# Transposing the right half of a graph's edge counts by DMA instead of on TensorE, in a four-layer graph network

## The chip, the cores and the metric

The kernel runs on one core of one Trainium2 chip. The metric is the device time of one execution in microseconds (us), lower is better. The core has five engines that run side by side, each with its own instruction stream: TensorE (PE in the profile; its weight loads are PEld), VectorE (DVE), ScalarE (ACT), GpSimd (POOL) and SyncE (SP), which here does nothing but issue DMAs. The engines are ordered among themselves by semaphores alone. TensorE writes to PSUM, eight banks of 128 x 512 float32; DVE and ACT read PSUM, a DMA does not.

## The reference, cut to what matters

Four graph layers over 1024 nodes of 512 features, each followed by a residual and a layer norm, with 16384 edges `(src, dst)`. The first layer, which the change touches, builds an adjacency matrix from the edges, made symmetric, and multiplies with it three times:

```python
def _L0_gnn_ref(x, edge_index, W, b, diffusion_weights):
    h = x @ W + b
    row, col = (edge_index[0], edge_index[1])
    adj = jnp.zeros((N, N), dtype=h.dtype)
    adj = adj.at[row, col].set(1.0)
    adj = adj.at[col, row].set(1.0)
    adj = adj + jnp.eye(N, dtype=h.dtype)
    row_sum = adj.sum(axis=1, keepdims=True)
    adj = adj / jnp.maximum(row_sum, 1.0)
    out = diffusion_weights[0] * h
    cur = h
    for i in range(STEPS):          # 3
        cur = adj @ cur
        out = out + diffusion_weights[i + 1] * cur
    return jax.nn.relu(out)

x = _layernorm(x + _L0_gnn_ref(x, edge_index, ...))
x = _layernorm(x + _L1_gnn_ref(x, W, b, src, dst, 1024))   # segment sum over edges, then @ W.T + b
x = _layernorm(x + _L2_gnn_ref(x, wc, wn, bias, edge_index))
x = _layernorm(x + _L3_gnn_ref(x, edge_index, Ws, Wb, a_w, a_b))   # attention, 8 heads
```

## The kernel before

Everything stays in SBUF. The edges become a dense matrix of counts: `c32` (float32, 8 tiles of 128 source nodes by 1024 destination nodes) is filled by one-hot matmuls of TensorE whose windows VectorE adds (L780, L1238), until about 66.9 us. Beside this TensorE computes `h = x @ W0` (L759), in float32.

Then comes the stage that the change touches, from 66.9 to 87.6 us:

- **Casts.** `c32` is cast to float16 in `cst` in pieces. The left half of the columns (0 to 511) is cast first, by ACT for tiles 0 to 2 (L517, which the profile shows under its helper's line, L453) and by DVE for tiles 3 to 7 (L1277). The right half (columns 512 to 1023) follows: tile 7 by ACT, tiles 0 and 1 by DVE (L1307), tiles 5 and 6 by ACT, tiles 2 to 4 by DVE (L1324). The semaphores `cst_act` and `cst_dve` count these casts, to 4 each.
- **Transposes.** `ct_block(t)` (L847) is eight transposes of 128x128 on TensorE (L853), which put column block `t` of all eight tiles into one PSUM bank (three banks in rotation); ACT copies that bank to `cts[:, t, :]` (L453, `cts<-ps`) and raises `cts_ready`. `cts` is the transposed count matrix in float16. Layer 3 reads it again, much later (L976).
- **Adjacency.** For `t` = 0 to 7 DVE waits for `cts_ready`, compares (L1318: an entry is 1 where either count is above 0, with the row sum), and adds the identity on the diagonal (L1322), which raises `adj_ready`. After tile 7 it computes the inverse degrees (L1325, L1326, semaphore `inv_r`) and the attention's weights (L1329 to L1331, semaphore `wa_lo`).
- **First multiplication, four banks.** TensorE goes over `j` = 0 to 7: it waits for `adj_ready` of tile `j` and issues 8 matmuls of 128x512 (L868) into the banks of tiles 6, 7, 3 and 4. Blocks 0 to 2 of the transposes are issued before this loop, block 3 before `j` = 0, and blocks 4 to 7 behind the matmuls of `j` = 1 to 4.
- **First multiplication, the other four banks** (L879, 64 matmuls), after `cts_ready` 8 and `wa_lo` 1. Then the second (L889, 128 matmuls) and third (L898) multiplications, and the later layers.

SP issues DMAs in the order of its program. After all of `h` is done it loads the weight matrices of the later layers, 1 MB each, into two staging halves: W1T and wc at once, wn and W3 as POOL frees the halves (`w_lo`, L395). ACT splits each into a high and a low part (`split_hi`, L453, `xTs<-xTs` and `big<-xTs`), from `inv_r` on, W1 and wc before it evicts the first multiplication. Later in the program SP issues 32 transposing DMAs (L340), each from one 128x512 float16 tile into four 128x128 blocks.

All of it is written out by hand: no scheduler moves anything. The order around the change is that of the code below.

Of the kernel before, what the change touches and what calls it, by code (L numbers as in the profile page):

```python
# [26 lines left out]
P = 128  # L27
N = 1024
D = 512
E = 16384  # L30
NT = N // P
# [19 lines left out]
ZERO_ACT = 6  # L51
CAST_COLS = ((0, 256), (256, 512), (512, 1024))
CT_BANKS = (0, 1, 5)
WINDOW_BANKS = (0, 1, 6, 7)

WSCALE = 64.0
# [40 lines left out]
def build(nc, x, xT, src, dst, W0, b0, dw, W1T, b1, wc, wn, b2, W3, W3T, b3, b3T, aw, ab, out):  # L97
    with ExitStack() as ctx:
# [10 lines left out]
        cst = sb("cst", [P, NT, N], F16)  # L109
        cts = sb("cts", [P, NT, N], F16)  # L110
# [147 lines left out]
        S = Semaphores()  # L258
# [38 lines left out]
        @block.sync  # L297
        def _(sp):
            sp.dma_start(e_dst, dst.rearrange("(g e) -> g e", e=GROUP)).then_inc(S["edges"], 16)
            sp.dma_start(e_src, src.rearrange("(g e) -> g e", e=GROUP)).then_inc(S["edges"], 16)  # L300
            sp.dma_start(first_i[:, 0, :], dst.rearrange("(a g e) -> a g e", a=1, e=GROUP)[:, :, 0],
                         allow_slow_non_contiguous=True).then_inc(S["edges"], 16)
            sp.dma_start(dwb[:], dw.rearrange("(a d) -> a d", a=1).broadcast_to([P, STEPS + 1])).then_inc(S["dw_in"], 16)
            sp.dma_start(w0raw, W0.rearrange("(k p) n -> p k n", p=P)).then_inc(S["w_in0"], 16)
            for half in range(2):
                nodes = slice(half * HALF, (half + 1) * HALF)
                sp.dma_start(xT32[:, :, nodes], xT.rearrange("(k p) n -> p k n", p=P)[:, :, nodes]).then_inc(S[f"xT_in{half}"], 16)
            sp.dma_start(w3t, W3T.rearrange("(k p) n -> p k n", p=P)).then_inc(S["w_in5"], 16)
            sp.dma_start(xcur[:], x.rearrange("(t p) d -> p t d", p=P)).then_inc(S["x_in"], 16)
            sp.dma_start(b0w, b0.rearrange("(a d) -> a d", a=1).broadcast_to([P, D])).then_inc(S["small_in"], 16)  # L310
            for i, b in enumerate((b1, b2, b3)):
                sp.dma_start(bb[:, i, :], b.rearrange("(a d) -> a d", a=1).broadcast_to([P, D])).then_inc(S["small_in"], 16)
            sp.dma_start(wbc[:], b3T).then_inc(S["small_in"], 16)
            sp.dma_start(abb[:], ab.rearrange("(a h) -> a h", a=1).broadcast_to([P, H])).then_inc(S["small_in"], 16)
            sp.dma_start(abc[:], ab.rearrange("(h a) -> h a", a=1)).then_inc(S["small_in"], 16)

            sp.wait_ge(S["const_ready"], 5)
            step = VCOL + H + 2
            flat = abT[:].rearrange("p k c -> p (k c)")
            for q in range(2):  # L320
                for u in range(2):
                    c0 = VCOL * u + q
                    sp.dma_start(flat[q * DH:(q + 1) * DH, c0:c0 + 3 * step + 1:step],
                                 aw.rearrange("(j q) (u p) -> q u p j", q=2, p=DH)[q, u],
                                 allow_slow_non_contiguous=True).then_inc(S["small_in"], 16)

            sp.wait_ge(S["h_done"], NT)
            for n, w in enumerate((W1T, wc, wn, W3)):
                if n >= 2:
                    sp.wait_ge(S["w_lo"], n - 1)  # L330
                sp.dma_start(stage[:, n % 2], w.rearrange("(k p) n -> p k n", p=P)).then_inc(S[f"w_in{n + 1}"], 16)
            for layer in range(1, 3):
                for t in range(NT):
                    name = ("xT_even", "xT_odd")[t % 2]
                    n = (layer - 1) * NT + t
                    sp.wait_ge(S["x_lo"], layer * NT + t + 1)
                    if n >= 2:
                        sp.wait_ge(S[name], n // 2 * TURNED)
                    for v in range(2):
                        sp.dma_start(xTs[:, v, :, t * P:(t + 1) * P], cur[:, 1, v, t, :],  # L340
                                     transpose=True).then_inc(S[name], 16)
            sp.wait_ge(S["uT_in"], 1)
            sp.dma_start(u_rows.rearrange("h (t p) -> (h t) p", p=P), uT).then_inc(S["u_kept"], 16)
            sp.wait_ge(S["u_kept"], 16)
            sp.wait_ge(S["wx_done"], NT)
            for h in range(2):
                sp.dma_start(uf[:, h], u_rows[h:h + 1].broadcast_to([P, N])).then_inc(S[f"uf_in{h}"], 16)
            for t in range(NT):
                if t in NORM_ACT:
                    sp.wait_ge(S["out_act"], NORM_ACT.index(t) + 1)  # L350
                else:
                    sp.wait_ge(S["out_dve"], NORM_DVE.index(t) + 1)
                sp.dma_start(out.rearrange("(t p) d -> t p d", p=P)[t], xcur[:, t, :]).then_inc(S["out_done"], 16)
            sp.wait_ge(S["out_done"], 16 * NT)
# [96 lines left out]
        def _(act):  # L451
# [66 lines left out]
                copy(cst[:, 0:CA, c0:c1], c32[:, 0:CA, c0:c1]).then_inc(S["cst_act"], 1)  # L518
            c0, c1 = CAST_COLS[2]
            copy(cst[:, 7:NT, c0:c1], c32[:, 7:NT, c0:c1]).then_inc(S["cst_act"], 1)  # L520
            for t in range(NT):
                act.wait_ge(S["ct_done"], t + 1)
                copy(cts[:, t, :], bank16(CT_BANKS[t % 3])).then_inc(S["cts_ready"], 1)
                if t == 2:
                    copy(cst[:, 5:7, c0:c1], c32[:, 5:7, c0:c1]).then_inc(S["cst_act"], 1)
# [64 lines left out]
            with act.Fori(0, NT // 2 - 1) as r:  # L590
                for i in (1, 0):
                    t = r * 2 + (2 - i)
# [12 lines left out]
            with act.If(flag(act, 2)):  # L605
# [23 lines left out]
                for a, n in enumerate(RELAYED):  # L629
                    h, j = n // NT, n % NT  # L630
# [83 lines left out]
        def _(pe):  # L714
# [48 lines left out]
            def quad(q):  # L763
# [7 lines left out]
                for w in (2 * q, 2 * q + 1):  # L771
                    pe.wait_ge(S["key_hot"], w + 1)
                    if w >= len(WINDOW_BANKS):
                        pe.wait_ge(S["win_free"], w - len(WINDOW_BANKS) + 1)
                    for c in (w % 2 * NC, w % 2 * NC + 1):
# [50 lines left out]
            with pe.If(flag(pe, 0)):  # L826
# [3 lines left out]
                with pe.Fori(0, NT) as a:  # L830
                    for b in range(2):
                        mm(ps[:, b, :], sel[:, H, :], iota_n[0:H, 0:HALF], start=True, stop=False)
                    with pe.Fori(0, NC * NG) as e:
                        n = a * (NC * NG) + e
# [12 lines left out]
            def ct_block(t):  # L847
                pe.wait_ge(S["cst_act"], (1, 2, 4)[chunk_of(t)])
                pe.wait_ge(S["cst_dve"], (1, 2, 4)[chunk_of(t)])
                if t >= 3:  # L850
                    pe.wait_ge(S["cts_ready"], t - 2)
                for j in range(NT):
                    ins = pe.transpose(bank16(CT_BANKS[t % 3])[:, j * P:(j + 1) * P], cst[:, j, t * P:(t + 1) * P], id16[:])  # L853
                ins.then_inc(S["ct_done"], 1)
# [7 lines left out]
            for j in range(NT):  # L862
                if j == 0:
                    ct_block(3)
                pe.wait_ge(S["adj_ready"], j + 1)
                for t in ORDER[0:OUTER]:
                    for v in range(2):
                        ins = mm(ps[:, t, :], adj[:, j, t * P:(t + 1) * P], cur[:, 0, v, j, :],  # L868
                                 start=j == 0 and v == 0, stop=j == NT - 1 and v == 1)
                    if j == NT - 1:  # L870
                        ins.then_inc(S["step_done"], 1)
                if 0 < j < NT - 3:
                    ct_block(j + 3)
            pe.wait_ge(S["cts_ready"], NT)
            pe.wait_ge(S["wa_lo"], 1)
            for t in ORDER[OUTER:NT]:
                for j in range(NT):
# [279 lines left out]
        def _(dve):  # L1157
# [74 lines left out]
            def add_window(w, first):  # L1232
                m = window(w // 2)
                dve.wait_ge(S["win_done"], w + 1)
                if w:
                    dve.wait_ge(S["win_free"], w)
                cells = c32[:, :, bass.ds(first.with_bounds(min_val=0, max_val=N - m), m)]
                tt(cells, cells, ps[:, WINDOW_BANKS[w % 4], 0:NT * m].rearrange("p (a w) -> p a w", w=m),  # L1238
                   ALU.add).then_inc(S["win_free"], 1)
# [41 lines left out]
            with dve.If(flag(dve, 0)):  # L1281
# [9 lines left out]
                with dve.Fori(0, NT) as a:  # L1291
                    with dve.Fori(0, CHUNKS) as e:
                        n = a * CHUNKS + e
# [13 lines left out]
            dve.tensor_copy(cst[:, 0:2, c0:c1], c32[:, 0:2, c0:c1]).then_inc(S["cst_dve"], 1)  # L1307

            for t in range(NT):
                dve.wait_ge(S["cts_ready"], t + 1)  # L1310
                if t == 0:
                    dve.wait_ge(S["cst_dve"], 3)
                    dve.wait_ge(S["cst_act"], 2)
                elif t == 2:
                    dve.wait_ge(S["cst_dve"], 4)
                elif t == 5:
                    dve.wait_ge(S["cst_act"], 4)
                stt(adj[:, t, :], cst[:, t, :], -1.0, cts[:, t, :], ALU.mult, ALU.is_lt,  # L1318
                    accum_out=deg[:, t:t + 1]).then_inc(S["adj_sum"], 1)
                dve.wait_ge(S["adj_sum"], t + 1)  # L1320
                diag = adj[:, t, t * P:(t + 1) * P]
                tt(diag, diag, id16[:], ALU.add).then_inc(S["adj_ready"], 1)  # L1322
                if t == 1:
                    dve.tensor_copy(cst[:, 2:5, c0:c1], c32[:, 2:5, c0:c1]).then_inc(S["cst_dve"], 1)  # L1324
# [61 lines left out]
            for k in range(1, STEPS):  # L1386
# [13 lines left out]
                for pos, t in enumerate(ORDER):  # L1400
                    n = (k - 1) * NT + pos + 1
# [79 lines left out]
            with dve.Fori(0, NT // 2 - 2) as r:  # L1481
                for i in (1, 0):
                    t = r * 2 + (2 - i)
# [278 lines left out]
```

## Time and profile before

| | us |
|---|---|
| median of 3 runs | 403.72 (403.42 to 404.16) |
| the profiled execution's own time | 403.67 |
| its span, first to last instruction | 401.8 |
| TensorE busy in the span | 370.4 (92%) |
| VectorE busy | 278.4 (69%) |
| ScalarE busy | 230.0 (57%) |
| GpSimd busy | 93.7 (23%) |
| chain that ended last: share of TensorE / VectorE / ScalarE | 74% / 14% / 3% |

The time of an execution is 1.9 us more than its span, so a change of the span is read as the same change of the time. The page gives busy time by engine; the chain of waits, followed back from the last instruction, tells which engine set the pace in which stretch; the timelines of single engines give the start and length of each instruction, and in brackets how long the engine sat idle before it and who released it. L numbers are lines of the kernel before.

### The profile page before, as it was taken

To read this page: it belongs to the slowest core of one execution; us is meant where nothing else is said; L and a number is where in the kernel's file an instruction comes from. 1 tells how busy PE (TensorE), PEld (TensorE's weight loads), DVE (VectorE), ACT (ScalarE), POOL (GpSimd) and SP (SyncE) were. 2 spreads that over 40 slices of the span, in tenths; PEclk is the share of its full clock that TensorE was granted. 3 is DMA by queue.
4 is the path that set the end of the run, shared out by engine and by line. 5 is a ranking of instruction groups with operands and counts; after the bars stand their busy time and mean duration, and the time that the engine had idled before them with its cause. 6 is when DMAs were issued, how large, how long until landed. Compare 5 with 4: busy or idle time off the path is not lost.

```text
span 401.8 us, 7998 instructions
## 1 busy us (share of the span) xinstructions
PE 370.4 (92%) x2704; PEld 216.0 (54%) x2704; DVE 278.4 (69%) x603; ACT 230.0 (57%) x390; POOL 93.7 (23%) x87
## 2 busy tenths in 40 slices
PE   1799889999999999999999999999798999999990
PEld 1254346444444444444444444444346889999990
DVE  7769998946996677024653222555798688999984
ACT  9789875566822145312562111246444999999444
POOL 4520000019940066500594000133100000012110
PEclk9999999999999999999999999999999999999996
DMA  5950004104100000000243000033202122210005
GB/s 180 390 178 2 1 0 160 52 0 148 64 0 2 1 0 3 2 0 0 42 91 78 0 2 2 2 76 79 54 1 63 46 68 93 97 64 2 4 3 212
DMA packets 27447, 22.71 MB, mean 57 GB/s; under 512 B 19536, under 2 KB 19728, under 8 KB 27408
## 3 DMA queue, kind: packets, MB, share of 16 engines
q1 hardware_dynamic: 26544, 19.06, 15.9%
q10 hardware_dynamic: 864, 3.15, 2.4%
q8 instruction: 23, 0.38, 0.4%
q14 instruction: 16, 0.13, 0.1%
HBM read 15.87 MB, written 2.13 MB: 45 GB/s over the span
## 4 chain that ended last, share of the span: by engine, by line
PE 74%; DVE 14%; issue 5%; ACT 3%; DVEq 2%; ACTq 0%
PE ps L726 15%; PE ps L1084 14%; PE ps L935 7%; PE ps L976 7%; PE ps L889 7%; PE ps L898 7%; PE ps L1025 7%; DVE c L1238 4%; PE ps L879 3%; PE ps L759 3%; PE ps L868 3%; DVE big L1473 2%; DVE adj L1219 1%; PE ps L780 1%; DVEq L1238 1%
## 5 line engine op out<-in xcount | busy, mean ns | idle before, releaser
L726 PE MATMUL ps<-big,xTs 128*128 128x512 f16 x384 | 84.4, 379 | 3.0 <-DVE cts L1460 3.0
L726 PEld LDWEIGHTS ps<-big,xTs 128*128 (+1 forms) x384 | 37.0, 98 | 47.0 <-issue 3.5
L635 ACT ACTIVATE big<-big,uvt 128x1024 bf16<-128x1024 f32 x55 | 59.0, 1153 | 0.0
L425 POOL TENSOR_TENSOR big<-xcur,big x24 | 27.8, 1157 | 119.6 <-ACT xcur L546 119.0
L545 ACT ACTIVATE big<-xcur,nmr,rstd x24 | 19.6, 815 | 38.8 <-DVE nmr L1344 38.8
L759 PE MATMUL ps<-big,xTs 128*128 128x512 f32 x64 | 35.3, 648 | 0.0
L453 ACT ACTIVATE big<-ps 128x512 f16<-128x512 f32 (+2 forms) x17 | 9.8, 574 | 39.9 <-PE ps L726 30.0
L1238 DVE TENSOR_TENSOR c<-c,ps 128x80 f32 (+31 forms) x64 | 23.3, 364 | 9.7 <-PE ps L780 5.6
L395 POOL TENSOR_TENSOR big<-xTs,big 128x2048 f16<-128x2048 f32 x4 | 16.3, 4086 | 58.8 <-ACT big L453 58.8
L1025 PE MATMUL ps<-big,cst 128*128 128x260 f16 x256 | 29.8, 275 | 0.0
L780 PE MATMUL ps<-adj,cts 128*128 128x80 f16 (+31 forms) x128 | 21.3, 271 | 8.9 <-DVE c L1238 4.8
L436 POOL TENSOR_TENSOR xcur<-xcur,c 128x512 f32<-128x512 f32 x6 | 7.1, 1182 | 94.6 <-DVE c L1557 94.6
L780 PEld LDWEIGHTS ps<-adj,cts 128*128 128x128 f16 x128 | 11.3, 108 | 31.7 <-issue 16.6
L935 PE MATMUL ps<-cst,big 128*128 128x512 f16 x128 | 27.8, 379 | 0.4 <-issue 0.4
L898 PE MATMUL ps<-big,adj 128*128 128x512 f16 x128 | 27.9, 379 | 0.0
L889 PE MATMUL ps<-big,adj 128*128 128x512 f16 x128 | 27.8, 379 | 0.0
L976 PE MATMUL ps<-big,cts 128*128 128x512 f16 x128 | 27.8, 379 | 0.0
L1025 PEld LDWEIGHTS ps<-big,cst 128*128 128x128 f16 x256 | 24.3, 96 | 4.8
L476 ACT ACTIVATE cts<-iota_lo,early 128x128 f16<-128x128 f16 x80 | 25.4, 393 | 0.4
L1219 DVE TENSOR_TENSOR adj<-adj,early 128x160 f16<-128x160 f16 (+31 forms) x64 | 22.3, 391 | 0.1
L453 ACT ACTIVATE big<-ps,invdeg 128x512 f16<-128x512 f32 x16 | 10.3, 688 | 19.1 <-PE ps L889 14.9
L935 PEld LDWEIGHTS ps<-cst,big 128*128 128x128 f16 x128 | 12.5, 98 | 15.7 <-issue 0.9
(206 smaller groups left out, 651.8 us busy)
## 6 DMA issues: line engine op xcount, KB each, us to landing
big<-u_rows ACTq DMA_DIRECT2D x6, 512.0 KB, 3.7
xTs<-in_xT SPq DMA_DIRECT2D x2, 1024.0 KB, 9.4
xcur<-in_x SPq DMA_DIRECT2D x1, 2048.0 KB, 17.8
out<-xcur SPq DMA_DIRECT2D x8, 256.0 KB, 2.5
big<-in_W SPq DMA_DIRECT2D x1, 1024.0 KB, 6.1
cts<-in_W3T SPq DMA_DIRECT2D x1, 1024.0 KB, 13.1
xTs<-in_W1T SPq DMA_DIRECT2D x1, 1024.0 KB, 5.4
xTs<-in_wc SPq DMA_DIRECT2D x1, 1024.0 KB, 8.2
```

The costliest lines, as they stand in the source:

```text
L425: pool.tensor_tensor(cur[:, 1, 1, t, :], xcur[:, t, :], cur[:, 1, 0, t, :], ALU.subtract).then_inc(S["x_lo"], 1)
L635: act.activation(above[:, a % AHEAD, :], uf[:, h % 2], ACT.Relu, scale=BIG, bias=vb[:, j, h:h + 1]).then_inc(S["above_in"], 1)
L726: return mm(bank, lhs(k)[a], rhs(k)[b], start=start and k == 0 and n == 0, stop=stop and k == KT - 1 and n == 2)
L759: ins = mm(bank, xT32[:, k, t * P:(t + 1) * P], w0raw[:, k, :], start=k == 0, stop=k == KT - 1)
L780: ins = mm(ps[:, WINDOW_BANKS[w % 4], 0:n], left, hot_key[:, r, w % 2 * NC * n:(w % 2 + 1) * NC * n].rearrange("p (k c) -> p k c", c=NC)[: ...
L889: ins = mm(ps[:, t, :], adj[:, j, t * P:(t + 1) * P], cur[:, 1, v, j, :], start=n == 0 and v == 0, stop=n == NT - 1 and v == 1)
L898: ins = mm(ps[:, t, :], adj[:, j, bass.ds(t * P, P)], cur[:, 0, v, j, :], start=n == 0 and v == 0, stop=n == NT - 1 and v == 1)
L935: ins = mm(ps[:, half * KT + k, :], cur[:, 1, v, j, k * P:(k + 1) * P], c[:, j, half * HALF:(half + 1) * HALF], start=c is cst and j == 0 ...
L976: ins = mm(ps[:, t, :], c[:, j, bass.ds(t * P, P)], cur[:, 0, v, j, :], start=c is cts and j == 0 and v == 0, stop=c is parts[-1] and j == ...
L1025: ins = mm(ps[:, DENSE_BANK[i], 0:4 * (DH + 1)], cst[:, j, t * P:(t + 1) * P], yh[:, j, v, 4 * half:4 * half + 4, DH + 1:YW], start=j == 0 ...
L1084: ins = mm(o, cz[h % CZ][:, j, t * P:(t + 1) * P], yh[:, j, v, h, :], start=j == 0 and v == 0, stop=j == NT - 1 and v == 1)
L1238: tt(cells, cells, ps[:, WINDOW_BANKS[w % 4], 0:NT * m].rearrange("p (a w) -> p a w", w=m), ALU.add).then_inc(S["win_free"], 1)
```

## The change

Tiles 0 to 3 of `cts` are made as before. Tiles 4 to 7, that is the right half of the columns of `cst`, are made by eight transposing DMAs, one for each tile `j` of `cst`: each reads 128x512 float16 of `cst[:, j]` and writes block `j` of the four tiles `cts[:, 4:8]`. SP issues them between the loads of W1T and of wc, in the order 0, 1, 7, 5, 6, 2, 3, 4, each group behind the cast that writes its source. TensorE's blocks 4 to 7 and ACT's four copies of them are gone. DVE waits ahead of tile 4 for all eight DMAs, and TensorE waits for `cts_ready` 4 instead of 8 ahead of the other four banks. The load of wc stands behind the eight DMAs.

```diff
+CT_PE = 4
@@ SP
             sp.wait_ge(S["h_done"], NT)
-            for n, w in enumerate((W1T, wc, wn, W3)):
+            def load(n):
                 if n >= 2:
                     sp.wait_ge(S["w_lo"], n - 1)
+                w = (W1T, wc, wn, W3)[n]
                 sp.dma_start(stage[:, n % 2], w.rearrange("(k p) n -> p k n", p=P)).then_inc(S[f"w_in{n + 1}"], 16)
+
+            def turn_counts(j):
+                sp.dma_start(cts[:, CT_PE:NT, j * P:(j + 1) * P], cst[:, j, CT_PE * P:N], transpose=True).then_inc(S["ct_turned"], 16)
+
+            load(0)
+            sp.wait_ge(S["cst_dve"], 3)
+            turn_counts(0)
+            turn_counts(1)
+            sp.wait_ge(S["cst_act"], 3)
+            turn_counts(7)
+            sp.wait_ge(S["cst_act"], 4)
+            turn_counts(5)
+            turn_counts(6)
+            sp.wait_ge(S["cst_dve"], 4)
+            turn_counts(2)
+            turn_counts(3)
+            turn_counts(4)
+            for n in range(1, 4):
+                load(n)
@@ ACT
-            for t in range(NT):
+            for t in range(CT_PE):
                 act.wait_ge(S["ct_done"], t + 1)
                 copy(cts[:, t, :], bank16(CT_BANKS[t % 3])).then_inc(S["cts_ready"], 1)
@@ TensorE
-                if 0 < j < NT - 3:
-                    ct_block(j + 3)
-            pe.wait_ge(S["cts_ready"], NT)
+            pe.wait_ge(S["cts_ready"], CT_PE)
@@ VectorE
             for t in range(NT):
-                dve.wait_ge(S["cts_ready"], t + 1)
+                if t < CT_PE:
+                    dve.wait_ge(S["cts_ready"], t + 1)
+                elif t == CT_PE:
+                    dve.wait_ge(S["ct_turned"], NT * 16)
```

The order of SP's instructions, from the load of W1T on (semaphores waited for in brackets; xTs is the staging memory). Before:

```order
L331 DMA xTs<-in_W1T 128x4x512 [waits h_done]
L331 DMA xTs<-in_wc 128x4x512
L331 DMA xTs<-in_wn 128x4x512 [waits w_lo]
L331 DMA xTs<-in_W 128x4x512 [waits w_lo]
L340 DMA_TRANSPOSE xTs<-big 128x4x128 [waits x_lo]
```

With the change:

```order
L333 DMA xTs<-in_W1T 128x4x512 [waits h_done]
L336 DMA_TRANSPOSE cts<-cst 128x4x128 [waits cst_dve]
L336 DMA_TRANSPOSE cts<-cst 128x4x128
L336 DMA_TRANSPOSE cts<-cst 128x4x128 [waits cst_act] x2
L336 DMA_TRANSPOSE cts<-cst 128x4x128
L336 DMA_TRANSPOSE cts<-cst 128x4x128 [waits cst_dve]
L336 DMA_TRANSPOSE cts<-cst 128x4x128 x2
L333 DMA xTs<-in_wc 128x4x512
L333 DMA xTs<-in_wn 128x4x512 [waits w_lo]
```

Eight transposing DMAs of the same shape as the later ones now stand between W1T and wc.

The order of TensorE's instructions, from the matmuls of `j` = 1 on. Before:

```order
L868 MATMUL ps<-big,adj 128x512 [waits adj_ready]
L868 MATMUL ps<-big,adj 128x512 x7
L853 MATMUL ps<-id16,cst 128x128 [waits cts_ready,cst_dve,cst_act]
L853 MATMUL ps<-id16,cst 128x128 x7
L868 MATMUL ps<-big,adj 128x512 [waits adj_ready]
L868 MATMUL ps<-big,adj 128x512 x7
L853 MATMUL ps<-id16,cst 128x128 [waits cts_ready,cst_dve,cst_act]
L853 MATMUL ps<-id16,cst 128x128 x7
```

With the change, where L889 is the line that was L868 and L898 the one that was L879:

```order
L889 MATMUL ps<-big,adj 128x512 [waits adj_ready]
L889 MATMUL ps<-big,adj 128x512 x7
L889 MATMUL ps<-big,adj 128x512 [waits adj_ready]
L889 MATMUL ps<-big,adj 128x512 x7
L898 MATMUL ps<-big,adj 128x512 [waits wa_lo,cts_ready]
```

The four blocks of transposes are gone from between the groups of eight matmuls, which now follow one another up to the first matmul of L898.

## Rows read from the trace of the kernel before

**Rows 1.** The page: the span, and busy time by engine
```profile
span 401.8 us, 7998 instructions
...
PE 370.4 (92%) x2704; PEld 216.0 (54%) x2704; DVE 278.4 (69%) x603; ACT 230.0 (57%) x390; POOL 93.7 (23%) x87
```

**Rows 2.** The chain of waits, 66.9 to 90 us: start us, us, engine, what
```profile
75.69 1.90 PE ps L868 x8
77.59 0.45 PE ps L853 x8
78.04 1.73 PE ps L868 x8
...
82.39 5.18 PE ps L868 x24
```

**Rows 3.** The chain of waits after 87 us, its longest pieces
```profile
87.57 13.81 PE ps L879 x64
101.38 27.63 PE ps L889 x128
```

**Rows 4.** Timeline of DVE: start, us, line, out<-in, [idle before <-releaser]
```profile
69.23 0.68 DVE L1307 CAST cst<-c 128x1024 f16<-128x1024 f32 x1
...
72.82 1.22 DVE L1324 CAST cst<-c 128x1536 f16<-128x1536 f32 x1
...
75.55 1.22 DVE L1318 SCALAR_TENSOR_TENSOR adj<-cst,cts 128x1024 f16<-128x1024 f16 x1
...
76.96 1.22 DVE L1318 SCALAR_TENSOR_TENSOR adj<-cst,cts 128x1024 f16<-128x1024 f16 x1
...
78.22 0.22 DVE L1322 TENSOR_TENSOR adj<-adj,id 128x128 f16<-128x128 f16 x1
79.13 1.23 DVE L1318 SCALAR_TENSOR_TENSOR adj<-cst,cts 128x1024 f16<-128x1024 f16 x1 [0.69 <-ACT cts L453]
...
83.48 1.23 DVE L1318 SCALAR_TENSOR_TENSOR adj<-cst,cts 128x1024 f16<-128x1024 f16 x1 [0.68 <-ACT cts L453]
...
85.81 0.33 DVE L1331 TENSOR_TENSOR wa<-abT,wa 128x160 f16<-128x160 f32 x1
```

**Rows 5.** Timeline of ACT, the same columns
```profile
71.62 1.06 ACT L453 ACTIVATE cst<-c 128x1024 f16<-128x1024 f32 x1
...
75.67 1.02 ACT L453 ACTIVATE cts<-ps 128x1024 f16<-128x1024 f16 x1 [2.07 <-PE ps L853]
...
85.38 1.91 ACT L453 ACTIVATE xTs<-xTs 128x2048 f32<-128x2048 f32 x1 [1.93 <-DVE invdeg L1326]
```

**Rows 6.** SP's transposing DMAs, L340, 196 to 216 us: ns min/median/max, starts
```profile
L340 SPq DMA_TRANSPOSE xTs<-big x15: 1189/1267/1313, 196.2 to 215.1; - x15
...
DMA to landing us min/median/max: 2.4/2.5/2.5
```

**Rows 7.** The same line, 279 to 283 us
```profile
L340 SPq DMA_TRANSPOSE xTs<-big x3: 1188/1268/2392, 278.2 to 281.3; - x3
```

**Rows 8.** A stretch: length, busy by engine, granted clock, DMA share, GB/s
```profile
197.50:198.00 0.50, 0.50 (x4) 0.26 (x3) 0.24 (x2) 0.00 (x0) 0.40 (x1) 1.00 1.03 209
```

**Rows 9.** DMA issues by what they load: KB each, us from issue to landing
```profile
xTs<-in_W1T SPq DMA_DIRECT2D x1, 1024.0 KB, 5.4
xTs<-in_wc SPq DMA_DIRECT2D x1, 1024.0 KB, 8.2
```

**Rows 10.** Stretches after TensorE's last matmul, the columns of rows 8
```profile
391.70:394.50 2.80, 0.00 (x0) 0.00 (x0) 2.56 (x13) 1.96 (x6) 0.00 (x0) 1.00 0.67 249
394.50:395.00 0.50, 0.00 (x0) 0.00 (x0) 0.47 (x2) 0.50 (x2) 0.00 (x0) 0.81 0.54 193
395.00:396.00 1.00, 0.00 (x0) 0.00 (x0) 0.89 (x5) 0.71 (x2) 0.00 (x0) 0.50 0.12 47
```

**Rows 11.** TensorE's float32 matmuls, L759, before 23 us and after
```profile
L759 PE MATMUL ps<-big,xTs x7: 682/1061/1220, 14.9 to 22.7; 128*128 128x512 f32 x7
...
L759 PE MATMUL ps<-big,xTs x53: 590/592/682, 22.7 to 60.0; 128*128 128x512 f32 x53
```

## The prediction

> **What bounds the kernel now.** I read the page first: TensorE is busy for 370.4 of 401.8 us [rows 1], so time is lost or won where TensorE waits. The chain of waits then says where it doesn't. From 75.69 us on, the chain is TensorE alone: groups of eight L868 matmuls of 1.73 us, between them three blocks of transposes of 0.45 us (77.59 us is the first of them), then 5.18 us of L868 without a block [rows 2], then L879 from 87.57 and L889 from 101.38 us without a gap [rows 3]. Whatever moves the end of L868 therefore moves the whole rest. Of a block's 0.45 us, three lie on the chain. The fourth (block 4) comes ahead of 75.69, where TensorE waits for VectorE anyway.
>
> VectorE's timeline shows who feeds TensorE. Tile 3 starts at 75.55 and tile 4 at 76.96, 1.41 us later, with no wait. From tile 5 on each waits some 0.69 us for ScalarE's copy (79.13, 83.48) [rows 4]. ScalarE's copy takes 1.02 us, and ScalarE sits idle for 2.07 us ahead of it [rows 5]. So VectorE could take a tile each 1.41 us, and TensorE takes one each 1.73 us: the pace is TensorE's, transposes included.
>
> **What the change removes.** TensorE loses four blocks; three on the chain are 3 x 0.45 = 1.35 us. ScalarE loses four copies, 4 x 1.02 = 4.1 us, worth nothing: it was idle before them, and its next work (the split of W1 at 85.38) waits for the inverse degrees, that is for VectorE [rows 5]. VectorE loses its waits of 0.69 us ahead of tiles 5 to 7. All of that counts only if the DMAs have landed when VectorE comes to tile 4, at 76.96 us.
>
> **What it adds: eight transposing DMAs.** The same kernel has the nearest row one could wish: 15 issues of L340 in one stretch, each from 128x512 float16 into four blocks at the same stride as here. Each holds SP for 1189 to 1313 ns, median 1267; from the first start, 196.2, to the last, 215.1 us, the 14 intervals are 18.9 us, 1.35 each, with short waits for GpSimd's tiles among them; one lands 2.4 to 2.5 us after its issue begins [rows 6]. I take an interval of 1.30 us, between the bare issue and the interval with waits.
>
> - The first waits for `cst_dve` 3, the L1307 cast, which ends at 69.23 + 0.68 = 69.91 us [rows 4]. Issue at 69.95.
> - The later sources are no brake: ScalarE's cast ends near 72.7 [rows 5], VectorE's L1324 at 74.04 [rows 4], while by SP's own pace the fourth DMA starts at 73.9 and the sixth at 76.5.
> - The eighth starts at 69.95 + 7 x 1.30 = 79.05 and lands at 79.05 + 2.5 = 81.55 us.
>
> VectorE waits at tile 4 for all eight. It stands ready at 76.96 and starts at 81.6, 4.6 us late. From the start of a tile to the end of its identity add it takes 78.22 + 0.22 - 76.96 = 1.48 us [rows 4], so TensorE gets tile 4 at 83.1. It has finished tile 3 at 75.69 + 1.90 + 1.73 = 79.3, so it stands idle for 3.8 us. Then come four groups of eight at 1.73 us (VectorE's 1.41 us keeps ahead), 6.9 us: L868 ends at 90.0 instead of 87.57. **The balance is +2.4 us**: 3.8 us of new wait less 1.35 us of transposes.
>
> **Is any of it taken up behind?** L879 waits for `wa_lo`, which came at 85.81 + 0.33 = 86.1, 2.7 us after tile 7 began at 83.48 [rows 4]. Tile 7 now begins at 81.6 + 3 x 1.41 = 85.8, so `wa_lo` comes at 88.5, ahead of 90.0. Nothing is gained or lost there. ScalarE's and GpSimd's weight splits, and VectorE's first corrections, all hang on the inverse degrees and move by 85.8 - 83.5 = 2.3 us, as TensorE does within 0.1; so L889, which needs them, meets what it met before. Behind it TensorE's chain has no gap [rows 3] in which a delay could vanish.
>
> **The moved load.** W1T's load goes first and landed after 5.4 us; wc, issued close behind it, after 8.2 [rows 9]. Now wc is issued behind the eighth transpose, at 80.4, and lands by 88.6 even at 8.2 us. ScalarE first splits W1 (two steps of 1.91 us from 85.38 + 2.3 = 87.7 [rows 5]) and needs wc at 91.5. Cost nothing, with 3 us of cover; if the load took over 11 us, the ScalarE evictions behind it would be late. wn and W3 wait for GpSimd as before and move with it. W1T has landed by 69.4 at that rate, before the first transpose.
>
> **Sum.** 403.67 (the profiled execution's own time, span 401.8 and 1.9 around it) + 2.4 = 406.1 us. The median of the runs, 403.72, is the same to 0.05. Bounds of the known terms: at the shortest issue, 1.189, and the shortest landing, 2.4, the last lands at 80.7 and the loss is 1.5; at 1.35 it lands at 81.9 and the loss is 2.8. One issue of 2392 ns stands in another stretch [rows 7]; one such here would add 1.1. This case alone holds 405.0 to 407.2.
>
> **Rivals.**
>
> *The clock falls in the new gap.* At the end of the kernel TensorE's last matmul ends near 391.7; the granted clock is still 1.00 up to 394.5, averages 0.81 in the next half microsecond and is 0.50 (1.2 GHz) after 395 [rows 10]. That is a fall some 3.1 us after the last matmul. The new gap is 3.8 us, the longest inside the kernel. Against it: the fall need not come at the same distance each time, and the gap ends only 0.7 us later. The price: in the kernel's first stretch float32 matmuls took 1061 ns where they take 592 later, from 14.9 to 22.7 us, 7.8 us of half rate though TensorE was at work [rows 11]. If the clock comes back 3 to 7.8 us after 83.1, half of that is lost, 1.5 to 3.9 us; I take 2.5, which gives 408.6 us. The Trainium skill (TensorE: Matmul & The Clock Gate, Part 1) has the clock go back to its lower level after idleness, and warns of waits for DMAs inside a kernel. Taken as sure, it would give 408.6 in place of 406.1; the trace has the fall only behind the last matmul, so I leave it a chance of 1 in 4.
>
> *The issue is not the pace, and it is faster.* In the burst from 197.5 to 198.0 us a transpose moved 209 GB/s at a DMA share of 1.03 [rows 8], so 128 KB took some 0.6 us, and the engines rested for the other half of each 1.30 us. If SP issued at the DMAs' pace, the last three (sources ready at 74.04) would start by 75.3 and land by 77.8: VectorE would be 0.8 us late, TensorE hardly, and all 1.35 us would be won, 402.3 us. The point at which it turns is worked back from the sum: the last landing at 81.55 - 2.4 = 79.15 us, an interval of 0.95 us. Against it stands the row of 15 with a minimum of 1.189 [rows 6]. The Trainium skill (Advanced Engine Details and Errata, X-Bar Transpose) calls transposing DMAs as fast as ordinary ones, with 350 to 400 GB/s to be expected. By that figure eight take 3 us and the time would be 402.3; the measured interval speaks against it. Chance 4 in 100.
>
> *Part of the delay is taken up or the landing comes near 79.1*: between 402.9 and 404.5, without a mechanism that the rows show. 6 in 100.
>
> *The change doesn't do what it says*: excluded by the order of instructions, which has eight transposing DMAs on SP, and four blocks gone from TensorE.
>
> **How the numbers follow.** The forecast has 65 in 100, the clock 25, the faster case 4, no change 6. Differences under 0.2% (0.8 us) can't be told from none: faster is below 402.9, slower above 404.5. Faster 0.04, same 0.06, slower 0.90. The range goes from just under the bound of the fastest issue, 404.9, into the clock's case, to 409.2, and leaves out the first two small cases and the far end of the clock's: about 2 in 10. The likeliest time is 406.1.
>
> **What would show it.** Right: eight transposing DMAs from about 70 us at 1.3 us each; VectorE idle for 4.6 us ahead of tile 4 with a DMA as releaser; one TensorE gap of some 3.8 us ahead of the fifth group of L868, no other change until the end, everything from L879 on 2.4 us later. Wrong in size: a granted clock under 1.00 between 82 and 91 us, or eight L868 matmuls taking more than 1.73 us. Wrong in kind: issue intervals below 0.95 us, VectorE's wait short, or a first transpose that starts long after 70 us, which would mean that SP waits for something I don't see.

## The result, and the profile after

The changed kernel takes 409.16 us (median of 4 runs, 408.61 to 409.63) against 403.69 (403.42 to 404.16): a ratio of 1.0137, interval 1.0125 to 1.0149. It is slower by 5.5 us, where the forecast had 2.4. The profiled execution took 408.77 us and its span is 406.9 us; before it was 403.67 and 401.8. Between these two the whole difference, 5.1 us, is in the span, and the sums below are worked out from them; the other 0.4 us is the distance of the profiled execution from the median.

The page of the changed kernel, its span and busy time by engine:

```profile
span 406.9 us, 7933 instructions
...
PE 371.9 (91%) x2672; PEld 216.2 (53%) x2672; DVE 278.0 (68%) x603; ACT 225.8 (55%) x386; POOL 93.5 (23%) x87
```

The other half of the comparison is [rows 1]: TensorE has 32 matmuls fewer and is busy for longer. That is a first sign that something made matmuls slower, not only later.

The chain of waits from 77.5 us on answers to [rows 2] and [rows 3] (start us, us, what):

```profile
76.59 1.26 SPq L336
...
77.90 2.04 SPq L336
...
79.98 2.48 DMA cts<-cst
...
82.48 1.24 DVE adj L1340 x2
...
83.75 0.23 DVE adj L1344
...
84.03 8.77 PE ps L889 x32
92.80 13.81 PE ps L898 x64
106.61 3.45 PE ps L908 x16
```

It runs through SP's queue (SPq), which had no place in the chain of before. L908 here is L889 of before, which began at 101.38, so it is 5.23 us late, and the span is 5.1 us longer. So the whole loss lies ahead of 93 us. Two pieces stand out: an issue of 2.04 us among issues of 1.26, and 32 matmuls that take 8.77 us. Before, 24 took 5.18, which makes 6.91 for 32.

The eight transposing DMAs, to be compared with [rows 6], and then VectorE's and TensorE's timelines at the wait, to be compared with [rows 4] (idle time before an instruction and its releaser in brackets):

```profile
L336 SPq DMA_TRANSPOSE cts<-cst x8: 1256/1266/2037, 70.0 to 80.0; - x8
...
DMA to landing us min/median/max: 2.5/2.5/4.0
```

```profile
75.74 1.22 DVE L1340 SCALAR_TENSOR_TENSOR adj<-cst,cts 128x1024 f16<-128x1024 f16 x1
...
82.48 1.22 DVE L1340 SCALAR_TENSOR_TENSOR adj<-cst,cts 128x1024 f16<-128x1024 f16 x1 [5.26 <-DMA cts<-cst]
```

```profile
84.03 8.77 PE L889 MATMUL ps<-big,adj 128*128 128x512 f16 x32 [4.53 <-DVE adj L1344]
92.64 13.98 PE L898 MATMUL ps<-big,adj 128*128 128x512 f16 x64
```

VectorE waits 5.3 us for a DMA, TensorE 4.5 us for VectorE. And the granted clock (the column after the five engines' busy times; then DMA share and GB/s):

```profile
83.00:84.00 1.00, 0.00 (x0) 0.00 (x0) 0.96 (x4) 0.00 (x0) 0.00 (x0) 1.00 0.84 174
84.00:85.00 1.00, 0.97 (x5) 0.50 (x6) 1.00 (x1) 0.00 (x0) 0.00 (x0) 0.95 1.04 403
85.00:86.00 1.00, 1.00 (x4) 0.36 (x3) 0.96 (x4) 0.00 (x0) 0.00 (x0) 0.50 1.02 395
...
88.00:89.00 1.00, 1.00 (x6) 0.37 (x5) 0.92 (x5) 0.41 (x1) 0.00 (x0) 0.84 0.00 0
89.00:90.00 1.00, 1.00 (x6) 0.46 (x5) 0.73 (x4) 1.00 (x1) 0.00 (x0) 1.00 0.00 0
```

The clock holds through the gap and falls to 0.50 (1.2 GHz) just after TensorE is back at work, until about 88.3. In the same microseconds the load of wc moves 400 GB/s, so the trace alone leaves two causes for the slow matmuls.

### The profile page after: what moved, and what is told of

Same layout as the page of the kernel before. It is cut to its first block, busy times and chain, and to the rows that moved or that the text cites. A ratio compares the mean times of both kernels' runs of the same rounds, so it can differ in the third digit from the quotient of the medians.

```text
span 406.9 us, 7933 instructions
## 1 busy us (share of the span) xinstructions
PE 371.9 (91%) x2672; PEld 216.2 (53%) x2672; DVE 278.0 (68%) x603; ACT 225.8 (55%) x386; POOL 93.5 (23%) x87
## 4 chain that ended last, share of the span: by engine, by line
PE 67%; DVE 8%; issue 2%; SPq 2%; ACT 2%; DMA 1%; DVEq 0%; ACTq 0%
PE ps L747 15%; PE ps L1103 12%; PE ps L954 7%; PE ps L995 7%; PE ps L917 7%; PE ps L908 7%; PE ps L1044 7%; PE ps L898 3%; PE ps L889 2%; DVE big L1495 2%; SPq L336 2%; DVE acc L1490 1%; DVE cts L1482 1%; DMA cts<-cst 1%; ACT xcur L567 0%
## 5 line engine op out<-in xcount | busy, mean ns | idle before, releaser
L908 PE MATMUL ps<-big,adj 128*128 128x512 f16 x128 | 27.8, 379 | 0.0
L474 ACT ACTIVATE big<-ps,invdeg 128x512 f16<-128x512 f32 x16 | 10.4, 685 | 21.1 <-PE ps L908 14.9
L1425 DVE SCALAR_TENSOR_TENSOR big<-ps,invdeg,big 128x512 f16<-128x512 f32 x16 | 11.9, 746 | 13.0 <-ACT big L474 13.0
```

The source lines that it names most:

```text
L908: ins = mm(ps[:, t, :], adj[:, j, t * P:(t + 1) * P], cur[:, 1, v, j, :], start=n == 0 and v == 0, stop=n == NT - 1 and v == 1)
```

## The experiments

The experiments ask three questions: what slowed the 32 matmuls, what held up one issue, and what the change would be worth if the DMAs came in time. In the diffs, L numbers are left out and lines of the changed kernel are the base (in e12_before_split those of the kernel before).

### e1_filler: TensorE kept at work in the gap

```diff
+                if j == CT_PE - 1:
+                    pe.wait_ge(S["cts_ready"], 2)
+                    for _ in range(18):
+                        mm(ps[:, 1, :], adj[:, 0, 0:P], cur[:, 0, 0, 0, :], start=True, stop=True)
```

> The changed kernel with 18 spare matmuls of 128x512 (into a free PSUM bank, result unused) on TensorE behind the matmuls of j = 3, where it stood idle for 4.5 us; 18 x 0.216 = 3.9 us of them fit. Theory (the granted clock fell because of the gap, and the four groups behind it took 8.77 us for 6.91): the clock stays at 1.00 through the stage, L868's last 32 matmuls take 6.9 us, and the time falls by 1.9 us, to about 407.3. Rival (the four groups were slowed by the load of wc, which moved some 400 GB/s in the same microseconds): they still take 8.8 us and the time stays at 409.2, since the load is untouched.

Measured 407.1 us (ratio to before 1.0086, 1.0070 to 1.0102), 2.1 us less than the change. TensorE's timeline, and the stretches behind the gap:

```profile
79.67 4.05 PE L896 MATMUL ps<-big,adj 128*128 128x512 f16 x18
84.31 7.08 PE L889 MATMUL ps<-big,adj 128*128 128x512 f16 x32 [0.60 <-DVE adj L1348]
91.23 13.98 PE L902 MATMUL ps<-big,adj 128*128 128x512 f16 x64
```

```profile
84.00:86.00 2.00, 1.69 (x8) 0.80 (x9) 1.93 (x5) 0.00 (x0) 0.00 (x0) 1.00 1.00 382
86.00:88.00 2.00, 2.00 (x11) 0.89 (x10) 1.97 (x4) 0.00 (x0) 0.00 (x0) 1.00 0.15 57
```

The load still moves 382 GB/s, the clock stays at 1.00, and the next line starts 6.92 us after the 32 matmuls do. So it was the gap that brought the clock down, and the load cost these matmuls nothing that shows. More work on TensorE made the kernel faster.

### e8_again, e7_shift_fetch and e9_move_fetch: the late issue

A 16 KB record of the instruction queue stands in the changed kernel's trace beside the late issue. The DMA queues between 78.4 and 78.6 us, and SP's issues around it:

```profile
q1 hardware_dynamic: 94, 0.02, 46.0%
q8 instruction: 1, 0.02, 32.8%
```

```profile
L336 SPq DMA_TRANSPOSE cts<-cst x1: 2037/2037/2037, 77.9 to 77.9; - x1
```

In the kernel before (at 77.1 us) and in every run with the eight DMAs up to here, that record comes some 28 to 30 matmuls, transposes counted, behind the start of the four-bank loop. That suggests that it goes with TensorE's place in its program. e8_again is the same kernel unaltered; e7_shift_fetch was meant to move the fetch.

```diff
+            for _ in range(60):
+                pe.nop(nofuse=True)
             pe.wait_ge(S["const_ready"], 4)
@@ after the second transposes
+            for _ in range(52):
+                pe.nop(nofuse=True)
```

> The changed kernel with 112 no-operations on TensorE in its first 9 us, where it waits for VectorE. They move TensorE's place in its instruction stream, and so the moments of its 16 KB instruction fetches, one of which lay at 78.5 us, just where the seventh transpose landed after 4.0 us and the eighth issue took 2.04. Theory (the fetch holds up the transposes): with no fetch between 72 and 81 us all eight issues take 1.27 us, the last lands at 81.6 to 81.8 and the time falls by 0.8 us; if the fetch falls elsewhere among them, the long issue follows it. Rival (the transposes' own traffic clogs after six or seven): the long issue stays the eighth.

> The changed kernel once more, unaltered, for one more execution of the profile. Theory: the late eighth issue comes again, because it goes with the place in TensorE's program; the half-rate stretch behind the gap comes again within a microsecond or is missing, since its time differs from one execution to the next.

e7_shift_fetch was a miss as an experiment: its trace holds exactly the instructions of the unaltered kernel, 2672 matmuls and as many weight loads, with no no-operation. It measured 409.45 us (1.0147, 1.0132 to 1.0163) and e8_again 409.64 in its single run, so both serve as repeats. In both the issue in the same place is the long one again, 2.2 us, and the clock is at 0.50 behind the gap again. In e8_again:

```profile
82.00:84.00 2.00, 0.00 (x0) 0.00 (x0) 1.36 (x3) 0.00 (x0) 0.00 (x0) 0.50 0.55 93
84.00:86.00 2.00, 1.85 (x5) 0.72 (x6) 1.97 (x5) 0.00 (x0) 0.00 (x0) 0.50 1.04 400
```

(The expectations miscount by one: the issue of 2.04 us, from 77.90, is the seventh, the eighth starts at 79.98; the transpose that landed after 4.0 us is the sixth.) e9_move_fetch used real instructions:

```diff
                     ct_block(3)
+                    pe.wait_ge(S["cts_ready"], 2)
+                    for _ in range(16):
+                        mm(ps[:, 1, 0:8], id16[:], cst[:, 0, 0:8], start=True, stop=True)
```

> The no-operations of e7_shift_fetch left no instruction in TensorE's stream (2672 matmuls and as many weight loads as without them, the fetch at the same place), so that run was a third execution of the same program. Here 16 spare matmuls of 8 columns (free bank, result unused) stand behind the transposes of block 3, where TensorE waits 0.9 us for VectorE. In every run the fetch came with the 28th to 30th matmul behind the start of L868; with 16 more matmuls and weight loads ahead it should come some 16 matmuls earlier, at 74 to 75 us. Theory (the fetch holds up the transposes): the long issue moves from the eighth to the fourth or fifth, and the last still lands at 82.4 to 82.6, time as before, 408.6 to 409.8. Rival (the transposes clog by themselves after seven): the eighth stays the long one, at 2.0 us.

Measured 408.93 us (1.0126, 1.0110 to 1.0141). SP's issues that were under way in 70 to 77 us and in 78 to 79 us, and the queues in 74.0 to 74.2 us:

```profile
L336 SPq DMA_TRANSPOSE cts<-cst x5: 1264/1267/2121, 69.9 to 76.1; - x5
...
L336 SPq DMA_TRANSPOSE cts<-cst x2: 1264/1266/1267, 77.4 to 78.7; - x2
```

```profile
q8 instruction: 1, 0.02, 30.4%
```

The fetch moved to 74.0 us. The long issue became the fourth, started at 73.9, the third landed after 4.0 us, and the seventh and eighth took 1.27. The last still landed at 82.5, so the time did not change. The instruction fetch holds up the transposes, wherever it falls among them; by what means is not shown.

### e2_no_dma and e5_act_zero: what is there to win

```diff
@@ e2_no_dma: no turn_counts; GpSimd
+            pool.memset(cts[:, CT_PE:NT, :], 0.0).then_inc(S["ct_zero"], 1)
@@ e5_act_zero: no turn_counts; ScalarE, behind its four copies
+            for t in range(CT_PE, NT):
+                copy(cts[:, t, :], zero[:].broadcast_to([P, N])).then_inc(S["cts_ready"], 1)
```

> The changed kernel without its eight transposing DMAs: GpSimd sets tiles 4 to 7 of the transposed counts to zero, in time for VectorE (so the adjacency and layer 3 miss those counts; the output is not the reference's). It shows what the change would be worth if the DMAs were free and early. Theory (the loss is the late landing and what it drags along): VectorE and TensorE run through without a gap, L868 ends 1.35 us earlier than before; but VectorE's first corrections, which start from the inverse degrees, then bound the second multiplication, so the time lands between 402.0 and 402.9. Rival (something else in the change costs, as the move of wc's load or the missing work of ScalarE): 404 or more.

> As e2_no_dma, tiles 4 to 7 of the transposed counts set to zero instead of transposed (the adjacency and layer 3 miss those counts), but by four copies on ScalarE, idle from 73.8 us on, one for each tile, and not by GpSimd, beside whose 3.3 us VectorE's and ScalarE's first casts were late and tile 3 started 1.3 us late. Theory (VectorE and TensorE run through; 1.35 us of transposes saved, nothing lost elsewhere): tile 3 starts at 75.6, L868 ends at 86.2, the time is 402.2 to 402.7. Rival (the gain is given back behind the stage, because VectorE's corrections set the second multiplication): L868 ends at 86.2, and the time is still 403.3 or more.

e2_no_dma measured 403.67 (1.0004, 0.9994 to 1.0013), over the 402.0 to 402.9 expected and short of the rival's 404. In its trace tile 3 of the comparison starts at 76.87, where before it was 75.55 [rows 4]. VectorE's casts ahead of it took longer (the pair at 66.8 us 2.82 us for 1.82, the one at 70.1 us 1.11 for 0.68) while GpSimd was at work, first with the fill of `cts`, 3.5 us from 64.4. That the one slowed the other is likely, but not tested alone. From tile 3 to the end of the loop it gains the 1.35 us that it lost ahead of it. e5_act_zero avoids that and measured 402.1 us (0.9973, 0.9960 to 0.9985):

```profile
75.54 10.53 PE L879 MATMUL ps<-big,adj 128*128 128x512 f16 x48 [0.51 <-DVE adj L1331]
85.91 4.26 PE L888 MATMUL ps<-big,adj 128*128 128x512 f16 x19
```

TensorE runs through, and L888 (L879 of before, 87.4 there) starts 1.5 us earlier; 0.15 of that was there at the start of the stretch (75.54 for 75.69). The rival, that VectorE's corrections would give it back, falls. The removed work was worth what the prediction said. Transposes that came in time would, by this run and the prediction's sum, have given 402.1 to 402.3, which is an estimate.

### e3_two_tiles, e4_one_tile and e10_three_tiles: fewer tiles by DMA

`CT_PE` is 6, 7 and 5, with TensorE's blocks up to it back in the loop.

```diff
-CT_PE = 4
+CT_PE = 6
@@ TensorE, behind the matmuls of j
+                if 0 < j < CT_PE - 3:
+                    ct_block(j + 3)
```

> Only tiles 6 and 7 are transposed by the eight DMAs (128x256 each), tiles 4 and 5 by TensorE as before. Theory (what counts is the last landing against the time at which VectorE comes to the first DMA tile): with the same 1.3 us an issue the DMAs land at 81.5 to 82.4, VectorE comes to tile 6 at 80.5, so it waits 1 to 2 us, TensorE 0 to 0.7; two blocks of 0.45 us are saved: 403.0 to 403.9. If an issue of half the blocks costs half, they land by 77.5 and the time is 402.9. Rival (the DMAs hurt by themselves, whatever the wait): over 405.

> Only tile 7 is transposed by the DMAs (128x128 each). VectorE comes to tile 7 at about 82.7 and finds it landed even at 1.3 us an issue with the late issue of 0.8 us. Theory: no wait for a DMA on VectorE, one block of 0.45 us saved, 403.2 to 403.4. Rival (DMAs hurt by themselves): over 405. The issue time of 128x128 beside 128x256 and 128x512 shows what an issue costs by size.

> Tiles 5, 6 and 7 by DMA (128x384 each), tile 4 by TensorE: the step between e3_two_tiles (403.25) and the change. Theory: the issues take 1.25 us whatever the size, the last lands at 82.3, VectorE comes to tile 5 at 78.3 and waits 4 us, TensorE waits 3 us and does three groups after that: L868 ends at 89.1 instead of 87.57, 405.2 with the clock up and up to 407.5 if it falls in that gap. Rival (the loss goes with the bytes that the DMAs carry): near 406.9, in proportion.

| tiles by DMA | us | ratio to before | VectorE's wait for the DMAs |
|---|---|---|---|
| 1 (e4) | 403.15 | 0.9987 (0.9978 to 0.9996) | none |
| 2 (e3) | 403.25 | 0.9991 (0.9982 to 1.0000) | 1.25 us |
| 3 (e10) | 406.7 | 1.0061 (1.0040 to 1.0082) | 3.65 us |
| 4 (the change) | 409.16 | 1.0137 (1.0125 to 1.0149) | 5.26 us |

The issues of e4_one_tile, then e3_two_tiles, then e10_three_tiles:

```profile
L336 SPq DMA_TRANSPOSE cts<-cst x8: 1194/1232/2226, 69.6 to 79.5; - x8
```

```profile
L336 SPq DMA_TRANSPOSE cts<-cst x8: 1236/1246/1769, 69.8 to 79.4; - x8
```

```profile
L336 SPq DMA_TRANSPOSE cts<-cst x8: 1246/1256/1910, 69.7 to 79.5; - x8
```

A quarter of the bytes costs 1.23 us an issue instead of 1.27, and each run has its one long issue. The last DMA lands between 81.8 and 82.5 us whatever it carries; what differs is when VectorE wants it. With one tile it never waits. With two, TensorE waits 0.21 us in all; the gain of either is half a microsecond, that of two at the edge of its interval. With three and four there is a gap behind which the clock is at 0.50. In e10_three_tiles TensorE waits 2.60 us:

```profile
83.44 6.97 PE L889 MATMUL ps<-big,adj 128*128 128x512 f16 x24 [2.60 <-DVE adj L1346]
```

```profile
83.40:85.00 1.60, 1.56 (x4) 0.58 (x5) 1.56 (x4) 0.00 (x0) 0.00 (x0) 0.50 1.04 403
```

The 24 matmuls would take 5.34 with the clock up, so 1.6 us come on top. The gap and that, less the three blocks saved (1.35), make 2.9 us, and 3.0 were measured (its five runs spread from 404.69 to 407.04, so the fall may not come each time). The time alone is also near the 406.9 of the rival. What speaks against a loss by bytes is that the last landing hardly moves, and the steps: from one tile to two 0.1 us, to three 3.5, to four 2.5.

### e6_useful_fill, e11_fill_split and e12_before_split: real work in the gap

```diff
+                if j == CT_PE - 1:
+                    pe.wait_ge(S["cts_ready"], CT_PE)
+                    for t in ORDER[OUTER + 1:NT]:
+                        for i in range(CT_PE):
+                            for v in range(2):
+                                mm(ps[:, t, :], adj[:, i, t * P:(t + 1) * P], cur[:, 0, v, i, :],
+                                   start=i == 0 and v == 0, stop=False)
@@ the other four banks
-                for j in range(NT):
+                for j in range(0 if t == ORDER[OUTER] else CT_PE, NT):
```

> The changed kernel with 24 of the 64 matmuls of L879 (banks 5, 0 and 1, source tiles 0 to 3) moved into TensorE's gap ahead of source tile 4, 5.2 us of work that is needed anyway. Theory (of the loss, the part of TensorE's gap can be bought back, but VectorE's corrections hang on the inverse degrees, 3.1 us later than before, and follow each 1.32 us): the clock stays at 1.00 behind the gap, the first tile of the second multiplication ends at about 107.3 instead of 104.8, time 406.1, about 1 us under e1_filler; TensorE waits for the corrections instead, and if the clock falls in that stretch the time is up to 408. Rival (only TensorE's gap counts): 402.5 to 403.

Measured 407.75 us (1.0090, 1.0068 to 1.0112; the runs lie between 405.77 and 409.0). Behind the filled gap the 32 matmuls take 6.91 us up to the next line's start, with the clock at 1.00. TensorE waits in the second multiplication instead, as the theory had it, and there the clock falls:

```profile
103.24 0.61 PE L915 MATMUL ps<-big,adj 128*128 128x512 f16 x2 [0.71 <-DVE big L1432]
104.55 0.86 PE L915 MATMUL ps<-big,adj 128*128 128x512 f16 x2 [0.71 <-DVE big L1432]
105.87 1.04 PE L915 MATMUL ps<-big,adj 128*128 128x512 f16 x2 [0.46 <-DVE big L1432]
```

```profile
105.00:107.00 2.00, 1.45 (x3) 0.13 (x2) 2.00 (x4) 1.88 (x2) 2.00 (x2) 0.50 0.29 110
107.00:111.00 4.00, 3.81 (x9) 1.31 (x10) 4.00 (x3) 3.56 (x3) 4.00 (x5) 0.50 0.02 4
```

Two matmuls each 1.32 us, with no idle time over 0.71 us, were followed by a fall as well. So VectorE's corrections were late next: ScalarE split two weight matrices, from 88.9 to 96.5 us, before it made the copies from which they start. e11_fill_split adds this to e6, and e12_before_split adds it to the kernel before:

```diff
-                for n in (2 * k - 1, 2 * k):
-                    split_hi(n, ...)
+                if k == 2:
+                    split(3)
                 for pos, t in enumerate(ORDER):
                     act.wait_ge(S["step_done"], (k - 1) * NT + pos + 1)
                     copy(cur[:, k % 2, 0, t, :], ps[:, t, :], invdeg[:, t:t + 1]).then_inc(S["step_hi"], 1)
+                    if k == 1 and pos == OUTER - 1:
+                        split(1)
+                split(2 * k)
```

> e6_useful_fill with ScalarE's order changed: it copies the first four banks of the first multiplication before it splits W1, and splits wc behind the other four, W3 behind the second multiplication. In e6_useful_fill VectorE's corrections began only at 97.2 us, behind both splits (7.6 us of ScalarE), and TensorE waited for them in the first tile of the second multiplication. Theory (with TensorE's gap filled, those corrections are what is late next): they begin at 92, the second multiplication starts at 100.3 without a wait, before 101.4 in the kernel before, and the time is 402.4 to 403.2, below both kernels. Rival (the corrections of the last banks, or the later splits, are late now): 404 or more, with TensorE waiting in L889 or L898 of the kernel before.

> The control for e11_fill_split: the kernel before with the same new order on ScalarE and nothing else. TensorE never waits for the corrections there, so theory says 403.4 to 404.0, no change; if it gains 0.8 us or more, the order and not the filled gap is what e11_fill_split gains by.

e11_fill_split measured 402.1 us (0.9960, 0.9946 to 0.9973), a little under the 402.4 expected at best, the control 403.72 (0.9999, 0.9990 to 1.0008). The chain of e11_fill_split is one run of TensorE from 75.72 on:

```profile
75.72 3.63 PE ps L894 x16
79.35 5.18 PE ps L903 x24
84.53 6.91 PE ps L894 x32
91.43 8.63 PE ps L910 x40
100.07 4.10 PE ps L920 x19
```

L920 (L889 of before) starts at 100.07 instead of 101.38, the 1.35 us of removed transposes, although the DMAs land no earlier. Of the versions run, only the filled gap together with the new order does it; the order alone is worth nothing. This version beats both kernels.

## Why the prediction was wrong

**The direction and its mechanism were right.** VectorE waits at tile 4, TensorE behind it, and nothing behind the stage takes the delay up (L908 and the span are late by 5.23 and 5.1 us). wc's moved load costs nothing: e1_filler's matmuls beside it are at full speed, and in the changed kernel ScalarE goes from W1's split to wc's at 92.35 us without a wait. ScalarE's saved work is worth nothing: it sat idle for 14.75 us ahead of its first split.

**The sum was mis-sized, 2.4 for 5.2 us.** The step that failed is the end of L868, 92.80 against the 90.0 of the forecast. Two terms of the sum were too small, and the rival that held most of the difference had too small a chance:

- *The last landing*, forecast 81.55, came at 82.46, 0.9 us late. The interval of 1.30 us was good (the six intervals from 70.02 to 77.90 are 1.31 each), but the seventh issue took 2.04 us with the instruction fetch. [Rows 7] was in the prediction as an issue of 2392 ns that "would add 1.1", and was left out of the sum without a look at what caused it. The same fetch record stands beside it in the trace before (its queues in 282.0 to 282.2 us below), and e9_move_fetch moved issue and fetch together.

```profile
q8 instruction: 1, 0.02, 39.2%
```

- *The groups behind the gap*, forecast 6.9 us, took 8.77. That is 1.7 us of half-rate clock, which the sum put at nothing, and 0.16 by which a row of matmuls lasts longer than the distance to the next row's start (7.08 for 6.92 us in e1_filler), which the sum left out too.
- *The rival on the clock* had the right mechanism, place (behind the gap) and nearly the right price: 1.5 to 3.9 us, measured from the start of the 32 matmuls to the next line at 1.7 in this profile, 2.3 in e8_again, 2.7 in e7_shift_fetch and 2.3 in e9_move_fetch, above the 6.92 of e1_filler. What was wrong is its chance of 1 in 4: it came in all four of these profiles. The gap expected, 3.8 us, was already longer than the 3.1 us after which the clock fell at the kernel's end [rows 10], and it became 4.5. Its 408.6 us was the better forecast, though in part by luck: it took 2.5 us for the clock where this profile shows 1.7, and held nothing for the 0.9 of the late landing. Its price also stood on weak rows: the granted clock of the kernel before reads 1.00 all through 14.9 to 22.7 us, so [rows 11] don't show that the slow float32 matmuls there were the clock's doing, and no row gives the 3 us of the lower bound. One point stays open: in this profile the clock fell 5.4 us after the last matmul, when TensorE was back, and in the other three 2.5 to 3.4 us after it, so the moment is not fixed by the gap alone. The rule of the Trainium skill that was weighed there (TensorE: Matmul & The Clock Gate, Part 1) held here: the clock was at 0.50 behind gaps of 4.5 to 4.8 us in all four profiles.

The median of 409.16 lies just inside the stated range, which ended at 409.2 to take in the clock's case; the forecast of 406.1 left that case out.

**The faster rival** failed where the prediction said it would, at the issue interval, and e5_act_zero shows its price right: 402.1 for 402.3. The bandwidth that the Trainium skill gives (Advanced Engine Details and Errata, X-Bar Transpose) was not reached by DMAs of this size: the eight starts took from 70.02 to 79.98 us, and an issue takes 1.23 us even for a quarter of the bytes.

## What to carry to other kernels

A transposing DMA here cost its issuing queue nearly the same time for 32 KB as for 128 KB: count issues, not bytes, and compare the last landing with the moment at which it is wanted. Gaps of 2.6 us and of 4.5 to 4.8 us in TensorE were followed by slow matmuls here, one of 0.21 us was not: price such a gap with the slow matmuls behind it, and put real work into it; then look for what is late next, here ScalarE's order. When a row in the trace is out of line with its neighbours, as the 2.39 us issue was, find out what stood beside it before leaving it out.

## What the runs showed of the hardware that was not expected

- The issue of a transposing DMA took 1.23, 1.25, 1.26 and 1.27 us for 128x128, 128x256, 128x384 and 128x512 float16.
- One 16 KB instruction fetch among these DMAs came with one landing of 3.7 to 4.2 us (medians 2.3 to 2.5) and one issue of 1.8 to 2.2 us (medians 1.23 to 1.27) in each of the ten profiles with the eight DMAs; in e9_move_fetch all three moved together.
- The clock fell not only after idleness. In the changed kernel's profile it was at 0.50 from 68 to 71 us as well, with TensorE shown busy ahead of it, by matmuls of 40 columns in float32 (L816). The kernel before was at 1.00 there in its one profile, but e12_before_split, whose instructions are the same up to there, averaged 0.52 in 68 to 71 us, so the change has nothing to do with it. It fell there, or some 3 us later (e2_no_dma), in seven of the fourteen profiles. It cost little: the first comparison started 0.19 us later in the changed kernel's profile than in that of before. What brings it about was not tested.

```profile
66.00:67.50 1.50, 1.50 (x16) 1.50 (x15) 1.19 (x3) 0.52 (x1) 0.00 (x0) 1.00 0.88 333
67.50:68.00 0.50, 0.50 (x5) 0.49 (x4) 0.50 (x2) 0.50 (x2) 0.00 (x0) 0.83 1.04 406
68.00:71.00 3.00, 3.00 (x29) 2.95 (x29) 2.80 (x4) 2.94 (x5) 0.00 (x0) 0.50 0.20 77
```
